# Loading the experts' weights after the inputs, and adding the output bias tile by tile: one attention and mixture-of-experts layer on one core

## The reference

```python
x = layernorm(x + attention(x, Wq, bq, Wk, bk, Wv, bv, Wo, bo))  # 16 heads of 16, causal; "@ Wo + bo" last
x = layernorm(x + ffn(x))
# ffn: scores = sigmoid(x @ gate_w); the best TOPK=2 of E=16 experts by scores + expert_bias
#      shared = (silu(x @ sg_w) * (x @ su_w)) @ sd_w
#      routed = sum over the 2 experts of weight_e * ((silu(x @ gate_e) * (x @ up_e)) @ down_e)
#      ffn(x) = shared + routed
```

## Time and profile before

| | value |
|---|---|
| median of 3 runs | 971.9 us (971.42 to 973.3) |
| the profiled execution | 973.44 us |
| its span, first to last instruction | 971.5 us |
| PE busy | 854.1 us, 88% |
| DVE busy | 661.0 us, 68% |
| ACT busy | 476.2 us, 49% |
| POOL busy | 298.9 us, 31% |
| granted clock of TensorE, mean | 0.943 |
| the eight chunk turns | from 602 to about 680 us |
| PE busy from 670 to 680 us, in the last of them | 8.01 us of 10 |

### The profile page before, as it was taken

How to read it: one execution, slowest core, us unless ns; L and a number is a source line. 1 busy time by engine, 2 the same in 40 slices (tenths; PEclk the granted TensorE clock), 3 DMA queues, 4 the chain that set the end, 5 groups by cost and what they waited for, 6 DMA issues and landing times. The chain is left out here.

```text
span 971.5 us, 17668 instructions
## 1 busy us (share of the span) xinstructions
PE 854.1 (88%) x5476; PEld 478.0 (49%) x5477; DVE 661.0 (68%) x1527; ACT 476.2 (49%) x686; POOL 298.9 (31%) x368
## 2 busy tenths in 40 slices
PE   7979799999999999999999997899987999999300
PEld 4635444444444444444444432787556787777200
DVE  6428778888888888888888860589891122366364
ACT  3523256666666666666666666365323444444100
POOL 3423312211122111221112211442577500454473
PEclk9979999999999999999999998899898999999755
DMA  8774855445754277524755001620126745667443
GB/s 287 189 198 145 163 67 63 104 99 66 132 65 103 32 131 131 67 37 98 130 66 67 1 2 48 213 65 23 65 99 213 228 140 152 208 201 220 157 124 98
DMA packets 82470, 114.06 MB, mean 117 GB/s; under 512 B 8944, under 2 KB 60400, under 8 KB 82416
## 3 DMA queue, kind: packets, MB, share of 16 engines
q1 hardware_dynamic: 57808, 78.01, 38.1%
q0 software_dynamic: 6720, 18.88, 6.1%
q10 hardware_dynamic: 17888, 16.41, 5.2%
HBM read 62.55 MB, written 50.33 MB: 116 GB/s over the span
## 5 line engine op out<-in xcount | busy, mean ns | idle before, releaser
L658 ACT ACTIVATE work<-ps 128x1024 f32<-128x1024 f32 (+3 forms) x384 | 293.8, 811 | 180.4 <-PE ps L725 180.2
L335 DVE TENSOR_REDUCE m_neg<-ps 128x1 f32<-128x512 f32 (+3 forms) x432 | 265.5, 663 | 25.2 <-PE ps L320 14.9
L629 POOL TENSOR_SCALAR_AFFINE_SELECT work<-work 128x512 f32<-128x512 f32 x128 | 81.2, 634 | 389.2 <-ACT work L658 384.7
L317 PE MATMUL ps<-stacks 96*128 96x512 bf16 (+3 forms) x528 | 151.0, 330 | 1.5 <-DVE m_neg L335 1.5
L725 PE MATMUL ps<-stacks 99*128 99x512 bf16 (+3 forms) x528 | 124.8, 329 | 6.2 <-PEq L371 4.7
L335 DVE TENSOR_REDUCE m_neg_late<-ps 128x1 f32<-128x384 f32 (+3 forms) x176 | 106.7, 636 | 26.5 <-PE ps L320 26.5
L740 PE MATMUL ps<-work,vg 128*32 128x512 f32 (+3 forms) x1056 | 112.5, 498 | 1.6 <-POOL work L629 1.6
L320 PE MATMUL ps<-mask_b,ident_b 128*128 128x128 bf16 x512 | 99.6, 221 | 0.0
L317 PEld LDWEIGHTS ps<-stacks 96*128 96x128 bf16 x528 | 49.6, 97 | 95.0 <-DVE m_neg L335 50.1
L1241 DVE TENSOR_TENSOR work<-work,ps 128x256 f32<-128x256 f32 x48 | 20.2, 421 | 108.2 <-ACT work L1060 108.2
L1419 PE MATMUL ps<-wgu,work 128*128 x384 | 92.5, 384 | 0.2 <-issue 0.2
(11 more groups left out here) (143 smaller groups left out, 1098.6 us busy)
## 6 DMA issues: line engine op xcount, KB each, us to landing
stacks<-qk_parts SPq DMA_DIRECT2D x132, 128.0 KB, 6.4
qk_parts<-work SPq DMA_DIRECT2D x32, 384.0 KB, 2.9
y_sorted<-work SPq DMA_DIRECT2D x8, 1536.0 KB, 10.0
work<-y_sorted SPq DMA_DIRECT2D x48, 256.0 KB, 3.1
z_sorted<-work ACTq DMA_DIRECT2D x48, 256.0 KB, 2.5
wgu<-qk_parts SPq DMA_DIRECT2D x60, 128.0 KB, 6.0
work<-in_xT SPq DMA_DIRECT2D x8, 512.0 KB, 5.2
work<-in_x SPq DMA_DIRECT2D x8, 512.0 KB, 3.9
```

The source lines that it names most:

```text
L317: mm = pe.matmul(dst, qs[r][0:KS, h0 + m, qt * P:(qt + 1) * P], ks[r][0:KS, h0 + m, half * CH:half * CH + w], start=True, stop=not diag)
L335: dve.tensor_reduce(dst, ps[:, bank, 0:heads * w].rearrange("p (h k) -> p h k", h=heads), AX.X, ALU.max, negate=True).then_inc(reduced, 1)
L629: pool.affine_select(out=blk_, in_=blk_, compare_op=ALU.is_ge, fill=0.0, base=0, pattern=[[0, GH], [1, P]], channel_multiplier=-1).then_in ...
L658: act.activation(probs[:, s + 2 * pair:s + 2 * pair + 2, off:CH], ps[:, SCORE_BANK + 2 * pair:SCORE_BANK + 2 * pair + 2, off:CH], ACT.Exp, ...
```

## The change

The load of `wgu` moves from behind the loads of x of chunks 0 and 1 to behind all eight, so that it is issued after the load of chunk 7, which waits for the residual of chunk 5. The addition of bo becomes four instructions of one tile (128x256) each, and each raises `xb_ready`. DVE waits for two tiles before the first half of the residual and for all four before the second, by `wait_apart`.

```diff
-                staggered(sp, [(0, load_x)], CHUNKS, turns=(0, 2))
+                staggered(sp, [(0, load_x)], CHUNKS)
                 sp.dma_start(wgu[:, :, :, :].rearrange("p e c n -> p (e c) n"),
                              gu_w.rearrange("e (c p) n -> p (e c) n", p=P)).then_inc(wgu_loaded, 16)
-                staggered(sp, [(0, load_x)], CHUNKS, turns=(2, CHUNKS))
...
                 def add_bias(c, b, r):
                     pool.wait_ge(x_loaded[r], 16 * b + 16)
-                    pool.tensor_tensor(xr[r], xr[r], bo_all[:, :].unsqueeze(1).broadcast_to((P, CT, D)),
-                                       ALU.add).then_inc(xb_ready, 1)
+                    for t in range(CT):
+                        pool.tensor_tensor(xr[r][:, t, :], xr[r][:, t, :], bo_all[:, :], ALU.add).then_inc(xb_ready, 1)
...
                 def residual(c, b, r):
                     wait_count(dve, yT_ready, c - 1)
                     wait_count(dve, y_saved, c - 1)
-                    dve.wait_ge(xb_ready, c + 1)
                     for i in range(2):
+                        wait_apart(dve, xb_ready, CT * c + 2 * i + 2, dve_waited)
                         dve.wait_ge(wo_ready, 2 * c + i + 1)
```

## The result

The changed kernel takes 966.0 us (median of 6 runs, 963.96 to 966.97) against 971.81 for the kernel before (6 runs, 970.89 to 973.3). The ratio is 0.9932, 95% interval 0.9922 to 0.9942: 5.8 us fewer, where 4.5 were forecast (967.4; range 963.0 to 971.4).

What follows compares the result with a forecast made beforehand. The chunk turns bound the kernel, with DVE losing time to a late load and to stalls under POOL's additions. Gains sum to 11.55 - 15s, 4.8 us at s = 0.45 per piece, less 0.3 for waits: 4.5, giving 967.4 (range 963.0 to 971.4).

Steps and rivals of the forecast that it cites:

- The path through the turns into the scatters: Eight chunk turns lead into POOL's first scatter: whatever they save moves the scatters and the end one for one.
- Part 1, gain 2.61 - 2s: Weights' load last: x of chunk 2 lands at 617.9, norm(0) pays two pieces, norm(1) starts at 623.48 + 2s.
- The price s of a piece: DVE's loss per quarter of POOL's addition of bo: taken as 0.45 us, between bounds 0.34 and 0.82.
- Who goes next, "they alternate": DVE's held operations and POOL's pieces take turns, so all pieces are paid in turns 4, 5, 6: gain 4.87 - 9s.
- The rival in which DVE keeps going: DVE's short gaps leave POOL's next piece no room; one piece's rest paid each time: gain 10.2 less 0.3, 962.0; 12%.
- that in which POOL does: POOL keeps going, its four pieces acting as one: stalls stay, gain 0.56 - 0.3, 971.6; 10%.
- That the pieces are dear: Each piece of POOL's addition costs DVE 0.6 to 0.8 us: gain 2.3 to -0.7, middle 0.8, 971.1; 13%.
- The new waits, 0.3 us: Separate 21 ns wait instructions before each residual half, 16 in all, cost between 0 and 0.3 us; 0.3 taken.
- Turn 6, gain 0.26: CAST comes at the first piece's end, so three pieces, 3s, are paid instead of a 1.61 us stall.
- The slower rival, instruction fetches stuck behind the 4 MB: Code after the loops queues behind the weights' load, PE stands 6 us: loss of 1.5, 973.4; 7%.

Runs made afterwards that it cites:

- e9: The changed kernel itself, unaltered, run again on another chip beside the kernel before; ratio 0.9942.
- e1: Kernel before with only the weights' load moved last, the addition of bo still one instruction; ratio 0.9989 to the kernel before.
- e4: Changed kernel with the addition of bo in eight pieces of 128 columns; ratio 0.9901 to the kernel before.
- e2: Kernel before with only the four pieces and their waits, the weights' load where it was; ratio 0.9987 to the kernel before.
- e5: Changed kernel, but SP issues the weights' load only after the residual of chunk 6; ratio 0.9953 to the kernel before.
- e11: The changed kernel itself, run a third time; 966.46 us against 972.51 for the kernel before, ratio 0.9928.
- e3: Weights' load last, addition of bo in one instruction that waits for DVE's norm of chunk c-2; ratio 0.9892 to the kernel before.
- e7: Weights' load last and the addition of bo left out, DVE waiting for x itself; ratio 0.9890 to the kernel before.

## Why the prediction was right, step by step

- The path through the turns into the scatters: right. The scatters moved by 6.0 us and the rest stayed at 283 us.
- Part 1, gain 2.61 - 2s: right. Norm(1) starts at 624.34, 624.38 was worked out; the addition of chunk 2 came into norm(0) between its second and third operation. That it did was partly luck: in e9 its load took 4.6 us, the addition came too late for norm(0), and nothing was paid there. e1 shows the 2s for what it is: with one whole addition there, turns 1 and 2 together gain 0.64 us.
- The price s of a piece: 0.45 was taken, 0.83 / 2 = 0.41 measured (2.21 - 1.38). The 0.45 was a choice between two bounds and not worked out, so that it came this near is luck. A piece takes 0.74 us, and 0.69 from one start to the next, where a quarter is 0.59, so POOL did become slower by it, from 2.35 to 2.9 us a chunk: the 0.06 us that the prediction read beside the columns of a memset are 0.15 in an addition (0.69 against 0.42 in e4, with half the columns). But 0.69 - 0.41 = 0.28 us of DVE's own operation lay under the hold (0.25 in the prediction), which left most of the added time without a price.
- Who goes next, "they alternate": right. In turns 4 and 5 the gain was 0.34 and 0.37 (0.28 each worked out). The rival in which DVE keeps going would have shown norms of little over 1.38 us behind the CAST (2.68 measured), and that in which POOL does a CAST of 2 us (0.41 measured). That the pieces are dear would have needed s from 0.6.
- The new waits, 0.3 us: mis-sized. From one half of the residual to the other, and from the norm to the residual, no time was added: 1.28 us for both halves, as before, and turn 7, in which no addition runs, took 6.95 us against 6.94.
- Turn 6, gain 0.26: it was 1.14, by luck. The prediction took it that the weights' load can't touch the load of chunk 7, which "stands ahead of it". In the profiled execution that load took 5.2 us with the weights behind it, so the addition came after the CAST. Where nothing delayed it, in e2 and e5, turn 6 took 8.52 and 8.51 us, where the prediction gives 8.81 - 0.26 = 8.55. Turn 6 and the waits are 1.2 of the 1.5 us between the profiled 6.0 and the 4.5 forecast; the rest is 0.05 to 0.1 in each of the other terms. Against the 8.81 before, e9 lost in turn 6 (9.12) and e11 gained nearly nothing (8.78); their T is 5.5 and 6.5 us below before all the same, by shorter turns 0 and 1.
- The slower rival, instruction fetches stuck behind the 4 MB: nothing of it. The weights' load covers 652.6 to 669.0, and PE was busy for 20.96 of the 22 us from 650 to 672.

In the view by windows of the changed kernel (stretch, length, busy time of each engine, granted clock, DMA share, GB/s):

```profile
650.00:672.00 22.00, 20.96 (x131) 17.61 (x131) 20.04 (x91) 14.44 (x17) 6.99 (x11) 1.00 0.68 216
```

## What to carry to other kernels

When an operation of DVE is longer than its like and no wait explains it, look at what POOL runs at that moment: a POOL addition on SBUF can hold a short cast or tensor-scalar until it is through, here 2 us for a CAST of 0.17. Splitting POOL's instruction helps as far as DVE runs out of such operations before POOL runs out of pieces, and as a smaller piece has a smaller price (0.41 us with 256 columns, 0.14 to 0.16 with 128). Moving it beside DVE work that it doesn't hold, here the additions from PSUM and the statistics, takes the stall away altogether: with the weights last, 12 us instead of 6. And an earlier transfer can be worth almost nothing by itself, because the work that it releases lands on something else.

## What the runs showed of the hardware

- DVE's TENSOR_SCALARs and CASTs and POOL's additions from SBUF to SBUF take turns, one instruction each, where both have some ready: back-to-back TENSOR_SCALARs of 256 columns went from 0.32 to about 0.74 us apart beside pieces of 256 columns, and to 0.46 or 0.47 beside pieces of 128 (e4), where a norm of four went from 1.38 to 2.02 us.
- DVE's additions from PSUM and its statistics are not held: 1.28 us for the residual's two additions, with POOL's addition beside them (e3) and without it (e7).
- A POOL addition from SBUF to SBUF takes about 0.15 us beside its columns: back to back, 128 columns are 0.42 us apart, 256 0.69, and 1024 2.30.
- The load of chunk 7, 512 KB, landed after 4.0 to 5.2 us in the eight profiles with 4 MB issued right behind it on the same queue, and after 3.7 or 3.8 in the four without. So a transfer issued later can delay an earlier one.
- From the scatters on, two chips took 64 us longer than others for the same program, with the turns alike; 25 to 29 us of idle time before one table load of ScalarE and 18 to 19 us on POOL are part of it. Nothing here shows the cause.
